# Score products of three attentions from split fp32r parts stacked in 32 or 64 rows a head group, brought there by DMA, in a gated cross-attention and expert kernel

## The reference, cut to what matters

```python
logits = einsum('bhqd,bhkd->bhqk', Q, K) + b          # block 0: 16 heads of 8, keys beyond seq_len masked by -1e12
scores = einsum('bthd,bshd->bhts', q, k) / 4           # block 2: 8 heads of 16, projected q and k, masked keys -inf
attn = einsum('bhnd,bhmd->bhnm', q * 8**-0.5, k)       # block 3: 16 heads of 8, 128 context keys and 128 own keys
weights = softmax(...); out = weights @ V
```

## Time and profile before

| | us |
|---|---|
| median of 3 runs | 1330.13 (1329.35 to 1359.78) |
| span of the profiled execution | 1321.6 |
| PE busy | 1159.9 (88%) |
| DVE busy | 829.9 (63%) |
| ACT busy | 543.4 (41%) |
| POOL busy | 296.4 (22%) |

### The profile page before, as it was taken

The page is one execution under the profiler, slowest core; times in us unless marked ns, Lnnn a source line. Parts: engine busy times, 40 slices in busy tenths (PEclk is TensorE's granted clock), DMA queues, the critical chain, the costliest instruction groups (busy, mean ns, idle before and its releaser), DMA issues.

```text
span 1321.6 us, 24304 instructions
## 1 busy us (share of the span) xinstructions
PE 1159.9 (88%) x9317; PEld 905.2 (68%) x9317; DVE 829.9 (63%) x1836; ACT 543.4 (41%) x963; POOL 296.4 (22%) x544
## 2 busy tenths in 40 slices
PE   4888999999999499997898998999558999999888
PEld 3666767777777477775676676777356778777655
DVE  4687458788887843333566579999834465551555
ACT  1455544333333233331334676667203455553412
POOL 3223011232221222225363013323320011100100
PEclk9989589999999599998899799999755697885989
DMA  4100000322100200000100024120000000000152
GB/s 153 50 3 3 3 24 27 106 82 70 70 25 1 88 1 0 1 0 33 34 3 3 16 56 115 49 88 32 1 1 2 11 3 3 3 3 2 36 197 95
DMA packets 23009, 49.33 MB, mean 37 GB/s; under 512 B 2800, under 2 KB 6000, under 8 KB 22768
## 3 DMA queue, kind: packets, MB, share of 16 engines
q1 hardware_dynamic: 22176, 46.99, 11.0%
q10 hardware_dynamic: 720, 0.80, 0.2%
HBM read 46.21 MB, written 1.25 MB: 36 GB/s over the span
## 4 chain that ended last, share of the span: by engine, by line
PE 69%; DVE 16%; issue 5%; ACT 5%; POOL 3%; DMA 1%; POOLq 0%; DVEq 0%; SPq 0%; ACTq 0%
PE bank L411 11%; PE bank L158 10%; PE bank L159 10%; PE bank L160 10%; PE bank L436 5%; PE bank L420 3%; DVE NM L490 3%; PE bank L1339 2%; PE bank L1536 2%; PE bank L1340 2%; PE bank L2106 2%; PE bank L374 2%; ACT EE L461 2%; PE bank L1899 2%; PE bank L2113 1%
## 5 line engine op out<-in xcount | busy, mean ns | idle before, releaser
L490 DVE TENSOR_REDUCE NM<-bank 128x2 f32<-128x512 f32 (+1 forms) x224 | 144.0, 685 | 135.3 <-PE bank L411 135.3
L411 PE MATMUL bank<-KT,QT 8*128 8x128 f32 (+2 forms) x1792 | 167.0, 333 | 47.0 <-DVE NM L490 20.3
L461 ACT ACTIVATE EE<-bank 128x512 f32<-128x512 f32 x224 | 121.5, 595 | 184.0 <-PE bank L420 183.8
L411 PEld LDWEIGHTS bank<-KT,QT 8*128 8x128 f32 (+2 forms) x1792 | 139.3, 229 | 83.5 <-issue 36.1
L420 PE MATMUL bank<-QT,KT 10*128 10x128 f32 (+1 forms) x1792 | 168.8, 336 | 1.8 <-ACT EE L461 1.7
L1316 ACT ACTIVATE SG<-bank,VC 128x512 f32<-128x512 f32 x128 | 88.2, 689 | 151.2 <-PE bank L160 151.2
L420 PEld LDWEIGHTS bank<-QT,KT 10*128 10x128 f32 (+1 forms) x1792 | 140.0, 231 | 7.2 <-issue 5.2
L1323 DVE SCALAR_TENSOR_TENSOR TT<-bank,VC,SG 128x512 f32<-128x512 f32 x128 | 96.0, 750 | 48.5 <-ACT SG L1316 45.3
L1376 ACT ACTIVATE SG<-bank,VC 128x512 f32<-128x512 f32 x128 | 87.8, 688 | 64.6 <-PE bank L160 62.3
L1393 DVE TENSOR_TENSOR HP<-SG,HP 128x512 fp32r<-128x512 f32 x128 | 95.7, 766 | 18.6 <-ACT HP L1381 15.9
L1233 POOL TENSOR_TENSOR ACC<-ACC,TM 128x512 f32<-128x512 f32 x48 | 65.4, 1364 | 181.8 <-DVE TM L1219 181.2
(11 more groups left out here) (258 smaller groups left out, 2425.7 us busy)
## 6 DMA issues: line engine op xcount, KB each, us to landing
CBS<-cw SPq DMA_DIRECT2D x96, 256.0 KB, 4.6
RAW<-in_w SPq DMA_DIRECT2D x8, 768.0 KB, 4.4
RAW<-in_w SPq DMA_DIRECT2D x8, 512.0 KB, 3.7
RAW<-in_w SPq DMA_DIRECT2D x4, 704.0 KB, 4.4
CTX<-in_ctx SPq DMA_DIRECT2D x4, 512.0 KB, 9.4
FK<-in_fkrow SPq DMA_DIRECT2D x1, 1024.0 KB, 4.7
RAW<-in_w SPq DMA_DIRECT2D x8, 128.0 KB, 2.7
out<-X SPq DMA_DIRECT2D x4, 256.0 KB, 2.3
```

Source lines behind the costliest of these rows:

```text
L411: ins = pe.matmul(self.K.PS[i][:, c:c + 128], qt1[32 * u:k, h:h + 128], kts1[kb][32 * u:k, h:h + 128], start=True, stop=True)
L461: act.activation(self.EE[:, b % 2, 2 * p + i, :], self.K.PS[2 + i][:, :], ACT.Exp).then_inc(sig("ee").sem, 1)
L490: dve.tensor_reduce(out, src, AX.X, ALU.max, negate=True).then_inc(sig("m1").sem, 1)
```

## The change

The score products get fp32r operands. Each query and key is split into a leading part (fp32r) and a rest (what is left of it, fp32r too), and the score is the sum of leading by leading, leading by rest and rest by leading. To have this in one product, the parts are stacked in the contracted rows: four rows for each channel of a head, of which row 0 holds the leading parts of both, row 1 the query's leading part and the key's rest, row 2 the query's rest and the key's leading part, and row 3 constants, masks (as a leading part and a rest) and the maxima's two parts. A head of 8 channels so has 32 rows, one of 16 has 64; the second has two row groups of 64 instead of four of 32.

SBUF partitions are interleaved by DMA alone: `sp_rows` issues three transfers for a batch's queries and three for its keys, of 64 KB each in pieces of 512 bytes, and `sp_largest` two for the maxima. Constant rows (`qc_in`, `kx_in`) and mask rows are written once a phase, also by DMA. In the first attention the keys are loaded already transposed and in stacked order, are split for four batches at a time (`act_keys`, `dve_keys`) and go out as twelve transfers (`sp_keys`); only x is transposed, once a batch. The second and third project into a dense layout: 2+1 and 2 products. The maxima are split by GpSimd (`pool_largest`), as are the second attention's keys and queries (`pool_split`). Normalisation goes from DVE to GpSimd (`pool_normal`), the output bias is added to X there. A fill of scores is now one bank, and PE may be two fills ahead. In the third attention one product covers the context's and the own keys of a head (256 columns) in the first scores.

```diff
     def init / __init__ of Heads
-        self.QT = sb(st, f"QT{tag}", [128, 4, self.W])
+        self.R = 4 * HD
+        self.U = 128 // self.R
+        self.NF = self.NH * NB // 4
+        self.QT = sb(st, f"QT{tag}", [128, 4, 512], F32R)
+        self.NMH = sb(st, f"NMH{tag}", [self.NH, 2, 2, 128], F32R)
...
+    def sp_rows(self, tile, i, parts, sem):
+        for k, src in enumerate(parts):
+            self.K.nc.sync.dma_start(tile[k:128:4, i, :].bitcast(F32).rearrange("p (g t) -> p g t", g=4), src.bitcast(F32)).then_inc(sem, 16)
+
+    def sp_largest(self, b):
         sp, sig = self.K.nc.sync, self.K.sig
-        for b in range(NBAT):
-            if b == 4:
-                early.sp()
-            sp.wait_ge(*sig("qt")(b + 1))
-            sp.wait_ge(*sig("nmt")(b + 1))
-            row = self.QT[self.HD + 1:128:32, b % 4, :]
-            sp.dma_start(row.rearrange("u (g q) -> u g q", g=self.NG),
-                         self.NMT[:, b % 2, :]).then_inc(sig("qm").sem, 16)
+        sp.wait_ge(*sig("nmh")(b + 1))
+        first = self.R - 5
+        for k in range(2):
+            row = self.QT[first + 4 * k:128:self.R, b % 4, :].bitcast(F32)
+            sp.dma_start(row.rearrange("u (g q) -> u g q", g=4), self.NMH[:, b % 2, k, :].bitcast(F32)).then_inc(sig(f"qm{b % 4}").sem, 16)
...
+    def pe_scores(self, j, b1, moving, b3, keys):
+        if do1:
+            if j == 0:
+                pe.wait_ge(*self.queries_in(b1))
+                self.pe_keys_in(b1)
+            if n1 >= 2:
+                pe.wait_ge(*sig("m1")(n1 - 1))
+        if do3:
+            if j == 0:
+                pe.wait_ge(*self.largest_in(b3))
+            if n3 >= 2:
+                pe.wait_ge(*sig("ee")(n3 - 1))
+        (u1, s1), (u3, s3) = self.head1(j), self.head2(j)
+        wide = 128 * self.NB
+        for m in range(4):
+            if do1 and m % self.NB == 0:
+                g = m if self.NB == 1 else 2 * s1 + m // 2
+                r = slice(self.R * u1, self.R * u1 + self.R - 5)
...
+                ins = pe.matmul(out, self.QT[r, b1 % 4, 128 * g:128 * g + 128], moving(r, 128 * g), start=True, stop=True)
...
             if do3:
+                r = slice(self.R * u3, self.R * u3 + self.R)
+                ins = pe.matmul(self.K.PS[2 + j % 2][:, 128 * m:128 * m + 128], keys(s3, r, 128 * m),
+                                self.QT[r, b3 % 4, 128 * m:128 * m + 128], start=True, stop=True)
...
 class Attn0
+    def sp_masks(self):
+        sp.dma_start(K.KT0[3:128:4, :, :].bitcast(F32), self.KX.bitcast(F32).unsqueeze(1).to_broadcast([32, NBAT + 4, 512])).then_inc(sig("kx_in").sem, 16)
+        sp.wait_ge(*sig("bm_lo")(1))
+        sp.wait_ge(*sig("kx_in")(16))
...
     def sp(self):
-        self.H.sp(self.early)
+        self.sp_masks()
+        self.sp_keys(0)
+        for s in range(0, self.LAST + 1):
+            b2 = s - 2
+            if s == 4:
+                self.early.sp()
+            if s < NBAT:
+                sp.wait_ge(*sig("ql")(s + 1))
...
+                H.sp_rows(H.QT, s % 4, [hi, hi, lo], sig(f"q{s % 4}").sem)
+            if s % 4 == 1 and s < 13:
+                g = s // 4 + 1
+                self.sp_keys(g)
+                if g + 1 < NGRP:
+                    self.sp_raw_keys(g + 1)
+            if 0 <= b2 < NBAT:
+                H.sp_largest(b2)
...
 class Attn2 (Attn3 has the same order)
     def sp(self):
+        for s in range(0, self.LAST + 1):
+            b2 = s - 2
+            if s == 4:
+                self.early.sp()
+            if 0 <= b2 < NBAT:
+                H.sp_largest(b2)
+            if s < NBAT:
+                sp.wait_ge(*sig("kql")(s + 1))
...
+                H.sp_rows(self.KT, s, [kh, kl, kh], sig(f"keys_in{s % 4}").sem)
+                H.sp_rows(H.QT, s % 4, [qh, qh, ql], sig(f"q{s % 4}").sem)
```

More of the change, by code:

```diff
@@ L358, in pool_keys, with head1 @@
[L358 to L363 removed]
+        return self.NF * n
+    def head1(self, j):
+        if self.U == 2:
+            return j, 0
+        return 2 * (j // (2 * self.NB)) + j % 2, j // 2 % self.NB
@@ new lines, in act_keys, with dve_keys @@
+    def act_keys(self, g):
+        K, sig, act = self.K, self.K.sig, self.K.nc.scalar
+        act.wait_ge(*sig(f"keys_raw{g % 2}")(16 * (g // 2 + 1)))
+        if g >= 2:
+            for i in range(4):
+                act.wait_ge(*sig(f"keys_in{i}")(48 * (g - 1)))
+        act.copy(self.KHL[:, g % 2, 0, :], self.KRAW[:, g % 2, :]).then_inc(sig("keys_hi").sem, 1)
+    def dve_keys(self, g):
+        K, sig, dve = self.K, self.K.sig, self.K.nc.vector
+        dve.wait_ge(*sig("keys_hi")(g + 1))
+        dve.tensor_tensor(self.KHL[:, g % 2, 1, :], self.KRAW[:, g % 2, :], self.KHL[:, g % 2, 0, :].bitcast(F32),
+                          ALU.subtract).then_inc(sig("keys_lo").sem, 1)
@@ L1829 @@
     LAST = NBAT + 4
+    BIAS = "bout"
     def __init__(self, K, st, early):
@@ L2133, in pe @@
                 read_b = [sig("on")(b4 + 1)]
+            scores(7)
     def act(self):
```

978 lines of the change are left out of this document (525 added, 453 removed).

## The result

The changed kernel takes 1514.95 us (median of 4 runs, 1512.60 to 1516.66). Against runs of the kernel before on the same chip the ratio is 1.1397, with a 95% interval of 1.1376 to 1.1418: 14% slower. (The ratio leaves out two slow runs of the kernel before, 1359.8 and 1375.4 us, which the median of 1345 us beside the changed kernel contains.) The forecast was 1439 us with a range of 1335 to 1500: the right way, but 76 us short and outside the range.

A forecast was written before the change was run, and what follows sets the result against it. The prediction took TensorE's work, priced by its clock, to bound all three attentions before the change, and transfer loops to be late after it: 91 + 33 - 15 = +109 us on 1321.6, 1431 in span, 1439 as median; range 1335 to 1500.

The forecast's parts named there:

- The second attention, 10.9 or 13.3 us a stage, 12.1 taken: Second attention: loop through SP's issues and landing, 10.9 us a stage at full clock, 13.3 at half; +91 us in all.
- I take the mean: Second attention: 12.1 us a stage taken between the full-clock and half-clock sums, though the lower level was called likelier.
- The first attention, +33: First attention: +5 for the steady loop, +11 for key issues ahead of the maxima, +17 for the start.
- Start +23.7 for +17: Start of the first attention: first score predicted at 38 us, where it stood at 21.27, so +17 us.
- 8.3, beside PE's 8.4: First attention at half clock: steady loop of 8.3 us a stage beside 8.4 us of TensorE's own work; before 8.0.
- The third attention, -15: Third attention: 12.0 us a stage against 13.37 before, -20 us, and 5 for its start.
- I take 12.0 for the same mixture: Third attention: 12.0 us a stage, assuming the clock changes between its levels as before; 9.7 at full clock, 14.2 at half.
- My sum for the lower level, 14.2: Third attention at half clock: TensorE's work decides the stage, 14.2 us.
- Full clock throughout: Rival: same loops in all three attentions with full clock kept, +45 us, 1375 us; chance 0.19.
- +22: First attention at full clock: its term in the rival that keeps full clock, +22 us.
- Cheap transfers: Rival: transfers cost SP and the loop next to nothing in all three attentions, -88 us, 1242 us; chance 0.13.
- Twice as dear scores: Rival: the two row groups of score blocks don't run side by side, 1553 us; chance 0.08.

The follow-up runs named there:

- a3_dense: Changed kernel with the third attention's two key and query projections each issued four times in a row into the same columns: 1489.6 us.
- the order experiment: Changed kernel with SP issuing the second attention's six key and query transfers ahead of the two of the maxima: 1466.4 us.
- a3_spread: Changed kernel with six redundant full-height fp32 products a stage in the third attention, one at a time between other products: 1541.7 us.

## Why the prediction went wrong

**What bounds each attention.** Right for the second: TensorE's first score of each stage waits for a transfer, summed 102.2 us. Right for the first only at its start, in the first stages and behind the two groups of twelve issues; in the other stages the first score waits 0.1 us at most, and TensorE's own work sets the pace. In the third, TensorE decides, as the sum for half clock had said: it waits for a transfer in the first four stages alone, 6.3 us in all.

**The second attention, 10.9 or 13.3 us a stage, 12.1 taken.** The mechanism was right and is shown by two experiments; the size was not: the steady stage is 14.2 us. The stretch from first score to maxima's issue took 7.7 us where the lower-level sum had 7.15, the way through ScalarE and GpSimd a little more than I gave it, and the eight issues with their gaps 5.0 us for 4.8. Issue (0.6) and landing (1.9) were as read from the earlier trace rows. What failed is the step "I take the mean": I had written that the lower level was the likelier there, and TensorE's work was at the lower level in every group; the upper level that the clock did reach fell into the wait. With 13.3 the term would have been 18 us larger. The pace from first to last transpose, which the sum multiplies by 15, was 13.4, so 13.3 would have met it, in part by luck: the steady stage is 0.9 us above it and the last two stages, 11.4 and 6.5 us, far below.

**The first attention, +33.** Start +23.7 for +17: the 1280 KB of constant rows landed 20.4 us after their issue. I had priced them by the 1 MB row transfer of the earlier trace rows. The twelve key issues cost 12.7 us in two waits, for 11. The stages cost more than the loop because "8.3, beside PE's 8.4" was a tie that TensorE lost: in the steady part it is busy 8.9 to 9.2 us of each stage, all at the lower level, and waits 0.7 us more for VectorE, so that the stages are 9.5 us and more; before, 7 of 16 groups ran at the upper level.

**The third attention, -15.** This step is the largest single miss, 38 of the 82 us between forecast and spans: "I take 12.0 for the same mixture" of clocks. There was no mixture: none of 61 groups at the upper level, and a pace of 15.5 us a stage. The change removed six of the eight full-height projections that stood in a row; a3_dense puts them back as dead work, and the clock rises with them and the kernel is 25 us faster. But the run was not all that had raised the clock in the kernel before. Of the six rises there between 1030 and 1200 us, three come behind it (1035.4, 1100.3 and 1151.5) and three (1045.6, 1059.3 and 1120.7) behind score blocks, three transposes and 32 products with the values, as here:

```profile
1056.25 0.47 PE L2089 MATMUL bank<-CP,XN 128*128 128x128 f32 x1
1056.52 0.42 PE L2092 MATMUL bank<-CP,ON 128*128 128x128 f32 x1
1056.73 0.42 PE L380 MATMUL bank<-CP,NM 128*16 128x128 f32 x1
1057.08 1.94 PE L436 MATMUL bank<-EE,VV 128*32 128x128 f32 x32
...
1059.31 0.27 PE L411 MATMUL bank<-KT,QT 8*128 8x128 f32 x2
```

The change altered this sequence too: score blocks on two row groups and not four, fills half as large, and the products with the values 16 at a time. No experiment put that back, or took the run alone out of the kernel before; how much of the lost clock is due to each is not known. My sum for the lower level, 14.2, was also short of the measured 16.7 of the steady stages. (The slowest stages of the kernel before, 16.4 and 16.7 us, were as long.) A fill of eight blocks takes 1.04 us there from its first start to the next operation, not 4 x 0.213 = 0.85: after each switch to another kind of product about 0.2 us are lost, and eight small fills lose it twice as often as the quarters of sixteen blocks. Eight fills are 8.3 us for the 6.8 that I gave them.

With the lower level in both attentions, 13.3 and 14.2 us a stage, my own sum comes to 1439 + 18 + 33 = 1490, inside the stated range. In the spans 31 us are left, terms that were too small: 7 at the start, 12 in the first attention, 8 in the second with what stands before it, 6 in the third with the same, less 2 at the end. They show as 25 because the median is 2.5 us above the profiled span here and not 8.5.

**The rivals.** Full clock throughout (1375) is the opposite of what happened; its "+22" for the first attention has no working, and by the rows there it is +25 (17 for the start, 11 for the issues, -3 for the stages). Cheap transfers (1242) is the farthest off and fell with the order experiment: eight issues are 5 us of the stage. The Trainium skill's sentence that issue time is usually small beside the transfer ("DMA: Bandwidth & Descriptors", Issuing engines are not separate DMA queues) does not fit transfers of 64 KB in 512-byte pieces: 0.6 us of issue for 1.9 of landing, and six in one queue. Twice as dear scores (1553) is nearer to 1515 than the forecast is, but its mechanism fell: 1.04/8 = 0.13 us a block at the lower level, where two row groups without overlap would give 0.21, and 0.59/8 = 0.07 at the upper.

The Trainium skill ("TensorE: Matmul & The Clock Gate", What's actually happening) ties the clock to how busy the engine has recently been. The rises in the second attention, each behind the work of a stage, fit that. In the third a busy engine is not enough: it was busy in 199.24 of 200 us of the third attention with the clock at its lower level throughout.

**What stays open.** What the clock looks at. That adding a run of full-height fp32 products raises it is shown in both kernels. What other work does is not: the kernel before has rises without such a run (above), a3_spread has three, and in the changed kernel score blocks on two row groups, transposes and 32-column products did not raise it in the third attention but stand ahead of rises, with a few full-height products, in the second.

## What to carry to other kernels

Before work is taken off a TensorE that bounds the stage, look at which of it runs ahead of each rise of the clock: the products that are saved may be the ones that pay for the speed of all others, and a saving at half the clock is none. A transfer of data that an engine could write itself costs its place in the issuing queue (0.6 us each here), so count all issues between the last input and the last transfer of a stage, put first in the queue what is ready first, and try more than one issuing engine. Where a forecast depends on two levels of a clock, work out the sum at the lower level for every stage, and do not average the two: here that alone gives 1490 us for 1439.

## What had not been expected of the hardware

- The same code can run at either level of the clock within one attention: five stages of 20.7 us at 0.50, then five of 11.8 to 13.6, mostly at the upper level (0.93 from 1330 to 1380 us), TensorE busy without a gap in both.
- The clock can rise just when there is nothing left to do: in the second attention the upper level stood for 30.7 of 180 us, TensorE busy in 3.9 of them.
- Redundant matmuls can make a kernel faster: 1326.4 to 1303.8 us in the kernel before, 1515 to 1479 in the changed one.
- A 1 MB transfer from 32 partitions held up the three issues behind it on the same engine for 9.1 us instead of 1.9.
- The clock column can say 1.00 where the durations say half; the length of 32 equal products (1.08 or 1.94 us) is the surer witness.
